# Two layers of window attention on one core: six q, k and v stacks, eight input tiles, one transfer of row maxima per unit, and a new table of slots

## The chip, the cores and the metric

The kernel runs on one NeuronCore of one Trainium2 chip. The metric is the device time of one execution in microseconds, from which the median of several runs is taken. A profiled execution has a time of its own; inside it lies the span, from the first to the last instruction of the core. TensorE has two clock levels, 1.2 and 2.4 GHz; the profile gives the granted one as a share of the upper (0.50 or 1.00, or a mean over a stretch).

## The reference, cut to what matters

There are 64 samples of 14x14 tokens with 192 channels, and two layers of the same kind. Each layer normalises groups of channels, makes q, k and v for 12 heads of 16 channels, adds relative position terms for rows and columns to the scores, takes the softmax over all 196 keys, and projects. The input is added to the result.

```python
qkv = hidden_states.reshape(B, HW, C) @ qkv_w.T + qkv_b
...
attn = jnp.einsum('bqd,bkd->bqk', q * scale, k)
rel_h = jnp.einsum('bhwc,hkc->bhwk', qr, Rh)
rel_w = jnp.einsum('bhwc,wkc->bhwk', qr, Rw)
attn = attn.reshape(B * nh, H, W, H, W) + rel_h[:, :, :, :, None] + rel_w[:, :, :, None, :]
attn = jax.nn.softmax(attn.astype(jnp.float32), axis=-1).astype(q.dtype)
out = jnp.einsum('bqk,bkd->bqd', attn, v)
out = out @ proj_w.T + proj_b
...
x = x + _L0_conv_ref(_gn(x), ...)
x = x + _L1_conv_ref(_gn(x), ...)
```

## The kernel before

**Units, slots, iterations.** One sample in one layer is a unit; there are 128. Every engine walks through the same iterations, and an iteration has 12 slots, one for each head. A step has a number, its place: a step at place 46 of unit n is done in slot 46 mod 12 = 10 of the iteration that lies 46 div 12 = 3 after the one of n. So the steps of some six units stand beside each other in one iteration, and in each iteration each step is done once, for some unit. The order of the instructions of an engine is fixed by the places and, within a slot, by the order in which the code asks for them. What an engine needs from another it waits for on a semaphore; all waits block the engine's own queue.

**The steps of a unit.** SP loads the input into `xa`; TensorE transposes it (`xT`); DVE and POOL make the statistics (`bn`, `mv`, `group`), with one small matmul `g` between them; POOL normalises and splits into two halves of 16 bits (`xn`, `xhi`, `xlo`). TensorE makes q and k (`qk0`, `qk1`) and v (`v`). ACT and DVE split q and k into `qk_hl`; SP writes them to DRAM (`qk_out`) and reads them back in another layout into the stacks `q_st` and `k_st` (`q_in`, `k_in`). The matmuls `rel0`, `rel1`, `rel2` make the position terms from `q_st`; ACT and DVE split them into `rel_hl`, and SP copies that into more rows of `q_st` (`rel`, four transfers).

**The two score passes.** For each head `ps_max` = q times k without the last row is made at MAX_AT + head (L525); DVE reduces it to the row maximum in `mx` (L718). TensorE transposes `mx` (`mT0` for the first six heads, `mT1` for the others, L480), ACT scales it into `mrow`, and SP copies `mrow` into the last row of `q_st` (`m0` and `m1`, L337). Then the same product with the last row, `ps_sc`, at EXP_AT + head (L538), has the maximum subtracted, and ACT takes the exponential into `probs` (L588). The matmul for head 0 waits for `m0` and that for head 6 waits for `m1`.

**The rest.** `ps_o` = v times probs (PV_AT, L557); ACT copies it to `o_sb`; `ot`, `on`, `oT` and `y` divide, transpose and project; POOL adds the input, which SP has loaded a second time into `xd`, and SP writes the result (`out`).

**Banks.** The jobs of TensorE other than L525, L538 and L557 share three PSUM banks. JOBS gives for each its place, name, bank and what tells that its bank has been read. `bank_free` lets a job wait until the job before it in the same bank has been read.

**Buffers.** `q_st`, `k_st` and `v_st` have four buffers each, `xa`, `xd`, `mrow` and most others two. SP's queue goes, in each iteration: `xa` (slot 0), `m0`, `qk_out`, `q_in` (slot 3), `k_in` (4), `xd` (7), `out` (9), `m1`, `rel` (10).

Of the kernel before, what the change touches and what calls it, by code (L numbers as in the profile page):

```python
# [58 lines left out]
UNROLL = 4  # L59

# [11 lines left out]
def attention_kernel(nc, x_in, w_all, b_qk, b_rows, rel, onehot, lo_rows, ident_in, gmat_in, out):  # L72
    with ExitStack() as ctx:
# [37 lines left out]
        q_st = [sb(f"q_st{i}", [128, HEADS, 2, HT], F16) for i in range(4)]  # L111
        k_st = [sb(f"k_st{i}", [128, HEADS, TOK], F16) for i in range(4)]
        v_st = [sb(f"v_st{i}", [HT, 2, HEADS, PW]) for i in range(4)]
# [5 lines left out]
        xa = pair("xa", [HT, 2, C])  # L119
# [18 lines left out]
        mrow = pair("mrow", [HEADS, 2, HT], F16)  # L138
# [6 lines left out]
        xd = pair("xd", [HT, 2, C])  # L145
# [52 lines left out]
        s_m = [sems(f"s_m{h}_") for h in range(2)]  # L198
# [13 lines left out]
        s_xd = sems("s_xd")  # L212
# [39 lines left out]
        JOBS = [(60, "y", 0, (s_yr, 1, 1)),  # L252
                (3, "qk0", 1, (s_qklo, 2, 1)),
                (3, "qk1", 0, (s_qklo, 2, 2)),
                (-9, "xT", 2, (s_xT, 1, 1)),
                (17, "rel0", 0, (s_rlo, 3, 1)),
                (41, "mT1", 2, (s_mrow, 2, 2)),
                (18, "rel1", 1, (s_rlo, 3, 2)),
                (-5, "g", 2, (s_g, 1, 1)),
                (56, "ot", 0, (s_on, 1, 1)),  # L260
                (20, "rel2", 1, (s_rlo, 3, 3)),
                (58, "oT", 2, (s_olo, 1, 1)),
                (10, "v", 0, (s_v, 1, 1)),
                (35, "mT0", 1, (s_mrow, 2, 1))]
# [44 lines left out]
        def _(sp):  # L309
# [36 lines left out]
            def iteration(unit, layer):  # L346
                for s in range(HEADS):
                    for half in range(2):
                        u = due(unit, s, SP_AT[f"m{half}"])
                        if u:  # L350
                            maxima(u, half)
                    u = due(unit, s, SP_AT["rel"])
                    if u:
                        wait(sp, s_rlo, u.n * 3 + 3)
                        for axis in range(2):
                            rows = RW if axis == 0 else 2 * SIDE
                            for half in range(2):
                                p, r0 = 64 * axis + 32 * half, R_REL + RW * axis
                                sp.dma_start(q_st[u.r][r0:r0 + rows, half * HH:half * HH + HH, :, :],
                                             rel_hl[u.r % 2][p:p + rows, :, :]).then_inc(s_rel[u.r], 16)  # L360
# [18 lines left out]
                    u = due(unit, s, SP_AT["xd"])
                    if u:  # L380
                        src, at = (x_in, u.n) if not layer_of(u, layer) else (x1, u.n - SAMPLES)
                        wait(sp, s_y, u.n - 1)
                        sp.dma_start(xd[u.r % 2][:, :, :], tokens(src[bass.ds(at, 1)])).then_inc(s_xd[u.r], 16)  # L383
# [6 lines left out]
                    if u:  # L390
# [3 lines left out]
                        wait(sp, s_xT_ps, u.n - 1)  # L394
                        sp.dma_start(xa[u.r % 2][:, :, :], tokens(src[bass.ds(at, 1)])).then_inc(s_x[u.r], 16)
# [7 lines left out]
        def _(pe):  # L403
# [14 lines left out]
            def job(name, unit, slot, layer):  # L418
# [6 lines left out]
                if name == "xT":  # L425
                    wait_dma(pe, s_x, u)
                    bank_free(pe, unit, name)
                    for c in range(2):
                        for h in range(2):
                            last = nc.tensor.transpose(ps[0:CC, c * TOK + h * HT:c * TOK + h * HT + HT],  # L430
                                                       xa[p2][:, h, c * CC:c * CC + CC], ident[0:HT, 0:HT])
# [20 lines left out]
                elif name.startswith("rel"):  # L452
# [7 lines left out]
                    for i in range(SIDE):  # L460
                        for axis in range(2) if i < rows else (1,):
                            w = 2 * (SIDE - 1 - (i if axis else a0 + i))
                            for half in range(2):
# [3 lines left out]
                                q = q_st[u.r][0:R_REL, half * HH:half * HH + HH, :, :]\  # L467
# [46 lines left out]
            def iteration(unit, layer):  # L514
                for s in range(HEADS):
# [3 lines left out]
                    if u:  # L519
# [394 lines left out]
```

## Time and profile before

| | |
|---|---|
| median of 3 runs | 2550.9 us (2547.81 to 2555.18) |
| the profiled execution | 2526.95 us |
| its span | 2525.2 us |
| TensorE busy in the span | 2178.0 us, 86% |
| VectorE (DVE) | 1434.6 us, 57% |
| ScalarE (ACT) | 1419.7 us, 56% |
| GpSimd (POOL) | 715.6 us, 28% |
| DMA, share of 16 engines | 33.8% |

The busy time of an engine is that of its instructions, whatever the clock, so TensorE's busy time holds matmuls at either level. The idle time in front of a group of instructions is put down to what released it. Names of tiles stand without their buffer number.

### The profile page before, as it was taken

The page shows a single profiled execution, that of the slowest core. Times are in us where ns is not written, and L with a number is a line of the kernel's source. Part 1 is how long each engine was busy: PE and PEld are TensorE (multiplying, and loading weights), DVE is VectorE, ACT ScalarE, POOL GpSimd, SP SyncE. Part 2 cuts the span into 40 slices and gives each one's busy share as a digit, 9 for nine tenths or more (in the row PEclk, how much of TensorE's full clock was granted, in tenths as well). Part 3 has the DMA queues.
Part 4 walks back from the last instruction along what each step waited for, and adds up shares of the span by engine and source line. Part 5 has one row for each costly group of instructions (what it writes and reads, how often), then busy time and mean ns, then how long its engine had stood idle before and what let it go on. Part 6 is the DMA issues. An engine that isn't in the chain of part 4 may idle for free.

```text
span 2525.2 us, 86928 instructions
## 1 busy us (share of the span) xinstructions
PE 2178.0 (86%) x35072; PEld 1815.6 (72%) x35072; DVE 1434.6 (57%) x3540; ACT 1419.7 (56%) x3329; POOL 715.6 (28%) x1796
## 2 busy tenths in 40 slices
PE   2888888888988888988988888988888888898897
PEld 2777777777777777776777777777777777777776
DVE  5655555565555556555555555655555655565554
ACT  1556555555655555655555555555555655565555
POOL 1322322232223223223222322332223222323220
PEclk9989888888888989989888988888888988998888
DMA  2433333333333334333333433333333333333331
GB/s 49 106 85 84 93 85 85 83 98 87 80 85 90 92 81 100 86 85 98 84 80 85 101 81 80 90 92 85 80 90 95 85 87 81 96 90 88 89 78 52
DMA packets 170599, 217.20 MB, mean 86 GB/s; under 512 B 29783, under 2 KB 138072, under 8 KB 170202
## 3 DMA queue, kind: packets, MB, share of 16 engines
q1 hardware_dynamic: 170202, 211.64, 33.8%
q8 instruction: 282, 4.62, 0.8%
q14 instruction: 115, 0.94, 0.1%
HBM read 117.00 MB, written 57.80 MB: 69 GB/s over the span
## 4 chain that ended last, share of the span: by engine, by line
PE 42%; DMA 30%; SPq 16%; DVE 5%; issue 3%; ACT 3%; POOL 1%; POOLq 0%; ACTq 0%
PE ps_m L413 21%; DMA q_st<-mrow 14%; DMA k_dram<-qk_hl 10%; PE ps_sc L538 8%; SPq L376 7%; PE ps_max L525 6%; DMA q_dram<-qk_hl 5%; DVE qk_hl L730 4%; SPq L383 3%; PE ps_m L501 3%; SPq L388 3%; PE ps_o L557 3%; ACT qk_hl L600 2%; SPq L342 2%; SPq L370 1%
## 5 line engine op out<-in xcount | busy, mean ns | idle before, releaser
L718 DVE TENSOR_REDUCE mx<-ps_max 98x2 f32<-98x392 f32 x1536 | 836.8, 562 | 433.1 <-PE ps_max L525 431.4
L588 ACT ACTIVATE probs<-ps_sc 98x392 f32<-98x392 f32 x1536 | 727.7, 495 | 536.6 <-PE ps_sc L538 505.5
L538 PE MATMUL ps_sc<-q_st,k_st 125*98 125x196 f16 x3072 | 568.7, 270 | 286.4 <-DMA q_st<-mrow 286.1
L525 PE MATMUL ps_max<-k_st,q_st 124*98 124x196 f16 x3072 | 580.4, 273 | 0.9 <-DVE mx L718 0.7
L538 PEld LDWEIGHTS ps_sc<-q_st,k_st 125*98 125x98 f16 x3072 | 352.7, 137 | 314.3 <-DMA q_st<-mrow 311.6
L525 PEld LDWEIGHTS ps_max<-k_st,q_st 124*98 124x98 f16 x3072 | 324.5, 135 | 204.7 <-issue 198.3
L802 POOL TENSOR_TENSOR msq<-mv 96x2 f32<-96x2 f32 x128 | 24.6, 192 | 1538.2 <-DVE mv L744 1538.2
L557 PE MATMUL ps_o<-probs,v_st 98*32 98x196 f32 x6144 | 389.0, 340 | 0.5 <-ACT o_sb L578 0.5
L636 ACT ACTIVATE rel_hi<-ps_m,is_lo 128x504 f16<-128x504 f32 (+1 forms) x384 | 225.8, 588 | 149.4 <-PE ps_m L474 137.3
L776 DVE TENSOR_TENSOR oT_lo<-ps_m,oT_hi 96x392 f16<-96x392 f32 x128 | 71.9, 562 | 415.5 <-ACT oT_hi L618 415.5
L474 PE MATMUL ps_m<-q_st,rel_st 64*32 64x36 f16 (+1 forms) x14336 | 238.2, 209 | 1.9 <-DVE rel_hl L769 1.6
L769 DVE TENSOR_TENSOR rel_hl<-ps_m,rel_hi 128x504 f16<-128x504 f32 (+1 forms) x384 | 216.2, 563 | 23.2 <-ACT rel_hi L636 6.5
L474 PEld LDWEIGHTS ps_m<-q_st,rel_st 64*32 64x32 f16 x14336 | 191.5, 101 | 46.1 <-DVE rel_hl L769 2.3
L413 PE MATMUL ps_m<-xn_hi,w_hi 98*128 98x196 f16 (+1 forms) x768 | 193.2, 252 | 10.4 <-POOL xn_lo L844 10.4
L413 PE MATMUL ps_m<-xn_lo,w_hi 96*128 96x196 f16 x768 | 192.2, 250 | 0.0
L730 DVE TENSOR_TENSOR qk_hl<-ps_m,qk_hl 128x392 f16<-128x392 f32 (+1 forms) x256 | 107.2, 460 | 149.5 <-ACT qk_hl L600 149.5
L413 PE MATMUL ps_m<-xn_hi,w_lo 96*128 96x196 f16 x768 | 191.6, 249 | 0.0
L557 PEld LDWEIGHTS ps_o<-probs,v_st 98*32 98x32 f32 x6144 | 134.4, 108 | 73.2 <-issue 1.0
L413 PE MATMUL ps_m<-w_hi,xn_lo 96*98 96x192 f16 x512 | 176.0, 344 | 0.0
L413 PE MATMUL ps_m<-w_lo,xn_hi 96*98 96x192 f16 x512 | 175.8, 343 | 0.0
L413 PE MATMUL ps_m<-w_hi,xn_hi 98*98 98x192 f16 (+1 forms) x512 | 175.6, 343 | 0.0
L413 PE MATMUL ps_m<-w_hi,oT_hi 98*98 98x192 f16 (+1 forms) x512 | 154.0, 301 | 2.7 <-DVE oT_lo L776 2.7
(72 smaller groups left out, 3338.3 us busy)
## 6 DMA issues: line engine op xcount, KB each, us to landing
q_st<-q_dram SPq DMA_DIRECT2D x128, 294.0 KB, 3.9
k_st<-k_dram SPq DMA_DIRECT2D x256, 147.0 KB, 3.9
q_dram<-qk_hl SPq DMA_DIRECT2D x128, 147.0 KB, 2.6
k_dram<-qk_hl SPq DMA_DIRECT2D x128, 147.0 KB, 2.7
q_st<-rel_hl SPq DMA_DIRECT2D x256, 73.5 KB
q_st<-rel_hl SPq DMA_DIRECT2D x256, 64.3 KB
xa<-in_x SPq DMA_DIRECT2D x64, 147.0 KB
xd<-in_x SPq DMA_DIRECT2D x64, 147.0 KB
```

Of the source, the lines that this page charges most:

```text
L376: sp.dma_start(k_st[u.r][2 * HD * part:2 * HD * part + 2 * HD, :, :], k_dram[u.r].rearrange("l d h c t -> d l (h c t)"))\
L383: sp.dma_start(xd[u.r % 2][:, :, :], tokens(src[bass.ds(at, 1)])).then_inc(s_xd[u.r], 16)
L413: last = nc.tensor.matmul(dst, weights(a, c, k), moving(b, c, k), start=n == 0, stop=n == len(terms) - 1)
L474: last = nc.tensor.matmul(to, rel_st[:, lay, axis, w:w + RW], q, start=True, stop=True)
L525: last = nc.tensor.matmul(ps_max[head % 2][0:HT, h * TOK:h * TOK + TOK], q_st[u.r][0:R_MAX, head, h, :], k_st[u.r][0:R_MAX, head, :], star ...
L538: last = nc.tensor.matmul(ps_sc[head % 2][0:HT, kt * TOK:kt * TOK + TOK], k_st[u.r][0:STACK, head, kt * HT:kt * HT + HT], q_st[u.r][0:STAC ...
L557: last = nc.tensor.matmul(ps_o[32 * j:32 * j + 32, 0:TOK], v_st[u.r][:, kt, head_of(head), :], p[:, kt, :], start=kt == 0, stop=kt == 1)
L588: nc.scalar.activation(probs[head][:, :, :], ps_sc[head % 2][0:HT, 0:2 * TOK].rearrange("p (k t) -> p k t", k=2), ACT.Exp, scale=1.0 / (QS ...
L636: nc.scalar.activation(rel_part(rel_hi[u.r % 2], n), rel_bank(n), ACT.Identity, scale=is_lo[:, 0:1]).then_inc(s_rhi, 1)
L718: nc.vector.reduce_max(mx[u.r % 2][:, head, :], ps_max[head % 2][0:HT, 0:2 * TOK].rearrange("p (q k) -> p q k", q=2), axis=AX.X).then_inc( ...
L730: nc.vector.tensor_tensor(qk_hl[u.r % 2][:, 1, at, :], ps_m[BANK[f"qk{j}"]][:, 0:len(tiles) * TOK].rearrange("p (c t) -> p c t", t=TOK), q ...
L769: nc.vector.tensor_tensor(rel_part(rel_hl[u.r % 2], n), rel_bank(n), rel_part(rel_hi[u.r % 2], n), ALU.subtract).then_inc(s_rlo, 1)
```

## The change

- `q_st`, `k_st` and `v_st` get six buffers, used in turn by the unit's number modulo six.
- `xa` gets eight buffers and is kept until POOL has added it to the result; the second load, `xd`, goes. A load of `xa` now waits for POOL's addition for the unit eight before it.
- The maxima of all 12 heads are transposed at once (`mT`, 24 rows in place of 12 twice), scaled by one ACT instruction and copied by one transfer, `m`. The matmul L538 waits for it at head 0 alone.
- All places are new: MAX_AT from 28 to 30, EXP_AT from 40 to 47, the jobs with their banks, the steps of POOL and SP. LEAD goes from 1 to 2, so there is one more iteration.
- At the start DVE fills two more `v_st` and the constant rows of two more `k_st`.

```diff
+VB = 6
+QB = 6
+XB = 8
...
-        LEAD, TAIL = 1, 6
-        MAX_AT, EXP_AT = 28, 40
-
-        PV_AT = {(0, 0): 44, (0, 1): 45, (1, 0): 49, (1, 1): 51, (2, 0): 54, (2, 1): 54}
+        LEAD, TAIL = 2, 6
+        MAX_AT, EXP_AT = 30, 47
+
+        PV_AT = {(0, 0): 52, (0, 1): 52, (1, 0): 55, (1, 1): 56, (2, 0): 59, (2, 1): 61}
...
-        JOBS = [(60, "y", 0, (s_yr, 1, 1)),
-                (3, "qk0", 1, (s_qklo, 2, 1)),
...
-                (41, "mT1", 2, (s_mrow, 2, 2)),
...
-                (35, "mT0", 1, (s_mrow, 2, 1))]
+        JOBS = [(-10, "xT", 1, (s_xT, 1, 1)),
+                (63, "ot", 0, (s_on, 1, 1)),
+                (4, "qk0", 2, (s_qklo, 2, 1)),
+                (5, "qk1", 1, (s_qklo, 2, 2)),
+                (65, "oT", 2, (s_olo, 1, 1)),
+                (18, "rel0", 0, (s_rlo, 3, 1)),
+                (42, "mT", 1, (s_mrow, 1, 1)),
+                (19, "rel1", 2, (s_rlo, 3, 2)),
+                (68, "y", 1, (s_yr, 1, 1)),
+                (-4, "g", 2, (s_g, 1, 1)),
+                (22, "rel2", 2, (s_rlo, 3, 3)),
+                (10, "v", 0, (s_v, 1, 1))]
...
-        POOL_AT = {"mv": -11, "group": -3, "xn": -1, "xhi": 0, "xlo": 0, "y": 63}
+        POOL_AT = {"mv": -8, "group": -5, "xn": -5, "xhi": -1, "xlo": 3, "y": 72}
...
-        SP_AT = {"m0": 39, "m1": 46, "rel": 22, "qk_out": 3, "q_in": 3, "k_in": 4, "xd": 55, "out": 69, "xa": -12}
+        SP_AT = {"m": 44, "rel": 23, "qk_out": 6, "q_in": 9, "k_in": 9, "out": 73, "xa": -22}
...
+                    u = due(unit, s, SP_AT["m"])
+                    if u:
+                        wait(sp, s_mrow, u.n + 1)
+                        sp.dma_start(q_st[u.n % QB][R_MAX:STACK, :, :, :], mrow[u.r % 2][:, :])\
+                          .then_inc(s_m[u.r], 16)
...
-                        wait(sp, s_xT_ps, u.n - 1)
-                        sp.dma_start(xa[u.r % 2][:, :, :], tokens(src[bass.ds(at, 1)])).then_inc(s_x[u.r], 16)
+                        wait(sp, s_y, u.n - XB + 1)
+                        sp.dma_start(xa[u.n % XB][:, :, :], tokens(src[bass.ds(at, 1)])).then_inc(s_x[u.r], 16)
...
-                        if head % HH == 0:
-                            wait_dma(pe, s_m[head // HH], u)
+                        if head == 0:
+                            wait_dma(pe, s_m, u)
...
-                        nc.gpsimd.tensor_tensor(yo[p2][:, :, :], yr[p2][:, :, :], xd[p2][:, :, :], ALU.add)\
+                        nc.gpsimd.tensor_tensor(yo[p2][:, :, :], yr[p2][:, :, :], xa[u.n % XB][:, :, :], ALU.add)\
```

On SP's queue, this is one iteration in the middle of the program before, with what each transfer waits for:

```order
L337 DMA q_st<-mrow 1x12x98 [waits s_mrow]
L342 DMA q_dram<-qk_hl 64x2x588 [waits s_qklo]
L342 DMA k_dram<-qk_hl 64x2x588
L370 DMA q_st<-q_dram 64x1x2352 [waits s_qd0]
L376 DMA k_st<-k_dram 32x1x2352 [waits s_kd0]
L376 DMA k_st<-k_dram 32x1x2352
L383 DMA xd<-in_x 98x2x192 [waits s_y]
L388 DMA x<-yo 98x2x192 [waits s_y]
L337 DMA q_st<-mrow 1x12x98 [waits s_mrow]
L359 DMA q_st<-rel_hl 32x1176 [waits s_rlo]
```

And this is one iteration of the same queue in the changed kernel:

```order
L335 DMA q_dram<-qk_hl 64x2x588 [waits s_qklo]
L335 DMA k_dram<-qk_hl 64x2x588
L344 DMA q_st<-mrow 1x24x98 [waits s_mrow]
L364 DMA q_st<-q_dram 64x1x2352 [waits s_qd0]
L370 DMA k_st<-k_dram 32x1x2352 [waits s_kd0]
L370 DMA k_st<-k_dram 32x1x2352
L353 DMA q_st<-rel_hl 32x1176 [waits s_rlo]
```

The second transfer of maxima stood behind the write of q and k to DRAM, their way back, `xd` and `out`; now the only one stands directly behind the write.

On DVE, before, these are the slots 2 to 6 of an iteration, from the reduction (L718) ahead of the split of q and k (L730) over the statistics (L739 to L744) to the position terms (L769):

```order
L730 TENSOR_TENSOR qk_hl<-ps_m,qk_hl 128x392 [waits s_kd0,s_qd0,s_qkhi]
L730 TENSOR_TENSOR qk_hl<-ps_m,qk_hl 128x196 [waits s_qkhi]
L718 TENSOR_REDUCE mx<-ps_max 98x2 [waits s_mT_ps,s_sm_ps]
L718 TENSOR_REDUCE mx<-ps_max 98x2 [waits s_sm_ps]
L739 BN_STATS bn<-xT 96x6 [waits s_xT]
L739 BN_STATS bn<-xT 96x6
L742 MEMSET anchor 96x1 [waits s_g_ps,s_bn]
L744 BN_AGGR mv<-bn 96x2 x2
L769 TENSOR_TENSOR rel_hl<-ps_m,rel_hi 128x6x84 [waits s_rhi,s_rel3]
```

In the changed kernel these are slots 5 to 8 on DVE (L713 is the split of q and k, L759 that of `oT`, L752 that of the position terms, L767 the copy after `g`):

```order
L701 TENSOR_REDUCE mx<-ps_max 98x2 [waits s_sm_ps]
L713 TENSOR_TENSOR qk_hl<-ps_m,qk_hl 128x196 [waits s_qkhi]
L759 TENSOR_TENSOR oT_lo<-ps_m,oT_hi 96x392 [waits s_y_ps,s_ohi]
L701 TENSOR_REDUCE mx<-ps_max 98x2 [waits s_mT_ps,s_sm_ps]
L752 TENSOR_TENSOR rel_hl<-ps_m,rel_hi 128x6x84 [waits s_rhi,s_rel3]
L701 TENSOR_REDUCE mx<-ps_max 98x2 [waits s_sm_ps]
L752 TENSOR_TENSOR rel_hl<-ps_m,rel_hi 128x6x84 [waits s_rhi]
L701 TENSOR_REDUCE mx<-ps_max 98x2 [waits s_sm_ps]
L767 COPY gsm<-ps_m 96x4 [waits s_gp,s_g_ps]
```

The split of `oT` now stands between that of q and k and those of the position terms, and four of the steps read or free the same bank 2.

## Rows read from the trace of the kernel before

**Rows 1.** The page: the span, its busy times and the clock in 40 slices.

```profile
span 2525.2 us, 86928 instructions
PE 2178.0 (86%) x35072; PEld 1815.6 (72%) x35072; DVE 1434.6 (57%) x3540; ACT 1419.7 (56%) x3329; POOL 715.6 (28%) x1796
PEclk9989888888888989989888988888888988998888
```

**Rows 2.** Who waited for whom: engine, tile, releaser, us, times, longest.

```profile
PE ps_sc L538 <- DMA q_st<-mrow: 286.1, 125, 3.7
```

**Rows 3.** Windows: length, busy time of each engine, granted clock, DMA.

```profile
108.88:125.14 16.26, 14.95 (x275) 12.14 (x275) 10.92 (x27) 10.83 (x26) 5.52 (x15) 1.00 0.40 105
125.14:2508.00 2382.86, 2099.26 (x33910) 1753.21 (x33910) 1362.26 (x3332) 1376.17 (x3231) 680.69 (x1699) 0.87 0.35 87
...
1219.00:1220.00 1.00, 1.00 (x8) 1.00 (x7) 0.47 (x1) 0.48 (x1) 0.00 (x0) 0.50 0.34 82
```

**Rows 4.** TensorE in order of time: start, length, what, [idle before].

```profile
1215.90 0.37 PE L525 MATMUL ps_max<-k_st,q_st 124*98 124x196 f16 x2
1217.77 0.56 PE L538 MATMUL ps_sc<-q_st,k_st 125*98 125x196 f16 x2 [1.50 <-DMA q_st<-mrow]
```

**Rows 5.** SP's queue in order of time, 1209 to 1216 us.

```profile
1209.63 0.64 SPq L342 DMA_DIRECT2D k_dram<-qk_hl  x1
1211.51 0.56 SPq L370 DMA_DIRECT2D q_st<-q_dram  x1
1212.46 1.96 SPq L376 DMA_DIRECT2D k_st<-k_dram  x2
1214.46 0.57 SPq L383 DMA_DIRECT2D xd<-in_x  x1
...
1215.53 0.81 SPq L337 DMA_DIRECT2D q_st<-mrow  x1
```

**Rows 6.** TensorE in order of time, pieces of two stretches at clock 1.00.

```profile
93.89 0.25 PE L413 MATMUL ps_m<-w_hi,xn_hi 98*98 98x192 f16 x1
...
94.89 0.33 PE L525 MATMUL ps_max<-k_st,q_st 124*98 124x196 f16 x2
...
1208.27 0.54 PE L557 MATMUL ps_o<-probs,v_st 98*32 98x196 f32 x8
1208.74 0.37 PE L525 MATMUL ps_max<-k_st,q_st 124*98 124x196 f16 x2
...
1209.56 0.67 PE L474 MATMUL ps_m<-q_st,rel_st 64*32 64x84 f16 x40
1210.15 0.25 PE L480 MATMUL ps_m<-ident,mx 98*12 98x98 f32 x1
```

**Rows 7.** From issue to landing of `k_st`, from the view of line L376.

```profile
DMA to landing us min/median/max: 2.8/3.9/5.0
```

**Rows 8.** Groups by line: busy us, mean ns | idle before, releaser.

```profile
L718 DVE TENSOR_REDUCE mx<-ps_max 98x2 f32<-98x392 f32 x1536 | 836.8, 562 | 433.1 <-PE ps_max L525 431.4
...
L769 DVE TENSOR_TENSOR rel_hl<-ps_m,rel_hi 128x504 f16<-128x504 f32 (+1 forms) x384 | 216.2, 563 | 23.2 <-ACT rel_hi L636 6.5
```

**Rows 9.** POOL in order of time: from the statistics to the split input.

```profile
1231.08 1.01 POOL L855 TENSOR_TENSOR yo<-yr,xd 98x384 f32<-98x384 f32 x1
1233.08 0.19 POOL L812 TENSOR_TENSOR msq<-gsm 96x2 f32<-96x2 f32 x1 [1.00 <-DVE gsm L784]
...
1236.88 0.93 POOL L844 TENSOR_TENSOR xn_lo<-xn,xn_hi 96x392 f16<-96x392 f32 x1
```

**Rows 10.** The start: DVE's fills, TensorE's first step, the first L538.

```profile
3.89 3.12 DVE L668 MEMSET v_st<- 98x768 f32 x4 [0.20 <-issue]
...
7.45 5.99 DVE L675 COPY k_st<-oh_f 61x196 f16<-61x196 f16 x48
...
33.22 0.89 PE L430 MATMUL ps_m<-ident,xa 98*96 98x98 f32 x4 [33.22 <-DVE yo L707]
...
85.49 0.53 PE L538 MATMUL ps_sc<-q_st,k_st 125*98 125x196 f16 x2
```

More of the change, by code:

```diff
@@ L108, in attention_kernel @@
         anchor = sb("anchor", [CC, 3])
-        q_st = [sb(f"q_st{i}", [128, HEADS, 2, HT], F16) for i in range(4)]
-        k_st = [sb(f"k_st{i}", [128, HEADS, TOK], F16) for i in range(4)]
-        v_st = [sb(f"v_st{i}", [HT, 2, HEADS, PW]) for i in range(4)]
+        q_st = [sb(f"q_st{i}", [128, HEADS, 2, HT], F16) for i in range(QB)]
+        k_st = [sb(f"k_st{i}", [128, HEADS, TOK], F16) for i in range(QB)]
+        v_st = [sb(f"v_st{i}", [HT, 2, HEADS, PW]) for i in range(VB)]
         def pair(name, shape, dt=F32):
             return [sb(f"{name}{i}", shape, dt) for i in range(2)]
-        xa = pair("xa", [HT, 2, C])
+        xa = [sb(f"xa{i}", [HT, 2, C]) for i in range(XB)]
         xT = pair("xT", [CC, 2, TOK])
@@ L137, in attention_kernel @@
         mx = pair("mx", [HT, HEADS, 2])
-        mrow = pair("mrow", [HEADS, 2, HT], F16)
+        mrow = pair("mrow", [2 * HEADS, HT], F16)
         probs = [sb(f"probs{i}", [HT, 2, TOK]) for i in range(HEADS)]
@@ L197, in attention_kernel @@
         s_mrow = sem("s_mrow")
-        s_m = [sems(f"s_m{h}_") for h in range(2)]
+        s_m = sems("s_m")
         s_sc_ps = sem("s_sc_ps")
@@ L347, in iteration @@
                 for s in range(HEADS):
[L348 to L351, printed above, removed]
+                    u = due(unit, s, SP_AT["m"])
[3 more added lines that the diff above has]
+                          .then_inc(s_m[u.r], 16)
                     u = due(unit, s, SP_AT["rel"])
@@ L375, in iteration @@
                         for part in range(2):
-                            sp.dma_start(k_st[u.r][2 * HD * part:2 * HD * part + 2 * HD, :, :],
+                            sp.dma_start(k_st[u.n % QB][2 * HD * part:2 * HD * part + 2 * HD, :, :],
                                          k_dram[u.r].rearrange("l d h c t -> d l (h c t)"))\
                               .then_inc(s_kst[u.r], 16)
[L379 to L383, printed above, removed]
                     u = due(unit, s, SP_AT["out"])
@@ L602, in iteration @@
                                            .rearrange("p (c t) -> p c t", t=TOK)).then_inc(s_qkhi, 1)
-                    for half in range(2):
-                        name = f"mT{half}"
-                        u = due(unit, s, AT[name] + ACT_LATER["mT"])
-                        if u:
-                            act.wait_ge(s_mT_ps, u.n * 2 + half + 1)
-                            before = unit((AT[name] + ACT_LATER["mT"]) // HEADS + 2)
-                            if active(before):
-                                wait_dma(act, s_m[half], before)
-                            nc.scalar.activation(mrow[u.r % 2][:, half, :], ps_m[BANK[name]][0:HEADS, 0:HT],
-                                                 ACT.Copy, scale=-1.0 / KS).then_inc(s_mrow, 1)
+                    u = due(unit, s, AT["mT"] + ACT_LATER["mT"])
+                    if u:
+                        act.wait_ge(s_mT_ps, u.n + 1)
+                        before = unit((AT["mT"] + ACT_LATER["mT"]) // HEADS + 2)
+                        if active(before):
+                            wait_dma(act, s_m, before)
+                        nc.scalar.activation(mrow[u.r % 2][:, :], ps_m[BANK["mT"]][0:2 * HEADS, 0:HT],
+                                             ACT.Copy, scale=-1.0 / KS).then_inc(s_mrow, 1)
                     u = due(unit, s, AT["oT"] + ACT_LATER["oT"])
@@ L640, in iteration @@
                         act.wait_ge(s_v_ps, u.n + 1)
-                        wait(act, s_o_ps, (u.n - 3) * GROUPS)
-                        nc.scalar.copy(v_st[u.r][:, :, :, 0:HD],
+                        wait(act, s_o_ps, (u.n - VB + 1) * GROUPS)
+                        nc.scalar.copy(v_st[u.n % VB][:, :, :, 0:HD],
                                        ps_m[BANK["v"]][0:HT, 0:2 * C]
@@ L666, in _ @@
                 nc.vector.memset(oT_hi[i][CC:CB, :, :], 1.0)
-            for i in range(UNROLL):
+            for i in range(VB):
                 nc.vector.memset(v_st[i][:, :, :, :], VS)
@@ L672, in _ @@
             dve.wait_ge(s_oh, 1)
-            for i in range(UNROLL):
+            for i in range(QB):
                 for head in range(HEADS):
```

48 lines of the change are left out of this document (14 added, 34 removed).

## The prediction, made before the changed kernel had run

> **What bounds the kernel now.** I read four views, in this order. The page first: TensorE is busy 86% of the span, DVE and ACT 57% and 56%, so none is full on average [rows 1]. Then the waits: on TensorE one line stands for nearly all idle time, L538 waiting for the transfer of the maxima, 286.1 us in 125 waits, 2.29 us each, one per unit [rows 2]. Then the windows. Between 108.88 and 125.14 us lies one full period, from the sixth-head wait of one unit to that of the next: 16.26 us, 14.95 of them busy, at clock 1.00. From 125.14 to 2508 us lie the 125 periods to unit 127's wait: 2382.86 / 125 = 19.06 us each, 2099.26 / 125 = 16.79 busy, 2.27 idle, at clock 0.87 [rows 3]. The same instructions take 1.84 us more of busy time, because for a part of every period TensorE runs at the lower level, 1.2 GHz [rows 3]: the wait that ends at 1217.77 is followed by a window at 0.50, with 8 matmuls in a microsecond [rows 3, 4]. So a period is 14.95 of work at 2.4 GHz, 2.27 of wait and 1.84 of what the wait leaves behind. The clock stays up with 1.31 us idle in the period (16.26 less 14.95) and falls in the period with 1.50 of wait [rows 3, 4].
>
> Last SP's queue, for why the maxima come late. `m1` is issued at 1215.53, and L538 goes on at 1217.77, 2.24 us later [rows 4, 5]. The transpose of an `mT` had begun at 1210.15 [rows 6]; from there the maxima lie ready, but SP is in the middle of the way of q and k over DRAM: the write at 1209.63, `q_in` at 1211.51 when the write has landed, `k_in` at 1212.46 for 1.96 us, `xd` at 1214.46, then `out`, then `m1` [rows 5]. The limit is a round trip through one in-order queue; no wait in the views is for a free stack.
>
> **The change part by part.**
>
> *The place of the maxima.* In the new table SP has only `qk_out` ahead of `m` in the half period that matters. I lay the period out from the start of slot 6 at clock 1.00, with pieces from rows: a group of PV 0.47 (1208.27 to 1208.74), a pair L525 and L538 0.41 with the changes of type (1208.74 to 1209.56 holds two), a `rel0` or `rel1` 0.59, a job of 12 split matmuls 1.0 (93.89 to 94.89) [rows 6]. `mT` begins after one pair and `rel0`, at 1.0. To the L538 of head 0 in slot 11 TensorE has: `rel1` 0.6, PV 0.5, `y` 1.0, `g` 0.1, PV 0.5, `rel2` 0.5, `v` 1.0, and four pairs and a half, 1.8. Sum 6.0, so head 0 is due at 7.0. ACT is at `mrow` at about 2.5 (it has the exponential of slot 6, the copy of `rel0` and the exponential of slot 7 ahead of it), SP issues at 2.6. With 2.24 from issue to use [rows 4, 5] the maxima are there at 4.8; with the longest landing of a far larger transfer, 5.0 [rows 7], at 7.6. I take the first, since it is this transfer, with 24 rows in place of 12. The stall of 2.27 goes whole; what is late next is nothing by 2.2 us. At the other bound 0.6 us of it stays.
>
> The Trainium skill (DMA: Bandwidth & Descriptors, section "Why a DMA increments its semaphore by 16 and not by 1") says that the first dimension of both sides sets over how many engines a transfer is split, the largest number up to 16 that divides both: by that 6 before (12 rows, 6 heads) and 12 now (24 rows, 12 heads), so landing would not be later and the sum stays. No row shows a transfer of 24.
>
> *The clock.* With no wait over 1.31 us left, the level stays up as in the stretch of 16.26 us, and the 1.84 goes too [rows 3]. Bounds: 1.84 back, or nothing back.
>
> *Work on TensorE.* One transpose less of 0.1 us; all else is the same. Period: 14.95 less 0.09 = 14.86.
>
> *Small new waits.* DVE has 10.92 us of work in a period, ACT 10.83 [rows 3], against 14.86, so neither is a bound on average; but slots 4 to 8 hold most of DVE's. I walk DVE through them with 0.56 for a reduction and about 0.63 for a long split of `rel` [rows 8]. It finishes the split of `qk1` at 0.8, where `mT` (same bank 1) wants to begin at 1.0; that of `oT` at 1.35, where `rel1` (same bank 2) wants 1.5; that of `rel1` at 3.9, where `g` (bank 2) wants 4.0. Three near ties, each with 0.1 to 0.2 us in hand. `g` also holds up the second half of PV behind it, and any such loss is a loss of the period. From below: 0. From above: each tie lost by one reduction that comes first, 0.56 us, some 1.1 for two of them. I take 0.1 us a period, since every tie falls on the good side.
>
> *POOL.* From `group` to `xlo` it takes 4.7 us (1233.08 to 1237.81), and the addition 1.0 [rows 9] now stands between `xhi` and `xlo`. Group starts at about 4.6, so `xlo` is done at 10.4 and `qk0` is due in slot 4, at 11.7: covered, 1.3 us in hand. If that cover went, `qk0` would wait, with everything behind it.
>
> *SP.* `xd` (0.57) and one of the two `m` (0.8) go [rows 5]. What moves: `q_in` and `k_in` to slot 9, nine slots ahead of `rel0`; `rel` to slot 11, four issues of about 0.7 each from 6.9 to 9.8, needed by L525 of head 0 at 14.86 + 0. With 3.9 to land 13.7, with 5.0 14.8 [rows 7]: just covered at both. `out` and `xa` now wait for POOL's addition, done at 9.4, and behind them in the queue is `qk_out`, due at 15.7: covered by 6 us. Six and eight buffers cost no time in the loop: they let a stack live from place 9 to 58, over four periods, which four buffers would not.
>
> *Start and end.* Two more `v_st` at 0.78 each and 24 more copies at 0.125 are 4.6 us ahead of TensorE's first step [rows 10]. From there to the first L538 it took 52.3 us for 49 places [rows 10]; now it is 57 places. At the same rate 8.5 us more; but the loop of the fill is freer (the transpose of the next unit no longer stands behind `qk0`), so between 0 and 8.5. I take 5. The end is of the same length.
>
> **Sum**, against the profiled execution: 125 x (19.06 - 14.86) = 525, and 3 for the two first periods (two waits of 1.3): 2525.2 - 528 = 1997. Plus 4.6, plus 5, plus 125 x 0.1 = 13: span 2020. The execution lies 1.75 above its span: 2022. The median before is 24 us above its profiled execution, which I put down mostly to the wait and the clock, which vary from period to period; 3 us of that stay: **2025 us**, 21% faster.
>
> **The rivals.**
>
> *Ties lost.* One or two of the bank waits on DVE bind in every period, for 0.2 to 1.1 us: 2050 to 2150 us. For it: DVE in slots 4 to 8 has next to no gap, and the walk sets no latency aside for semaphores. Against it: DVE's dense part now ran next to TensorE without waits of TensorE that the views would show but one.
>
> *The maxima come late in part.* Landing at 5 us: 0.6 us a period, 2100 us with the clock up. For it: one transfer now serves head 0 as well, so every head depends on it, and it shares the engines with the write of k. Against it: 2.24 us measured among heavier traffic [rows 4, 5].
>
> *The clock does not stay up.* Tiny waits, one at each near tie, would hold TensorE at the lower level for as long as now: 1.84 x 125 = 230, so 2255 us. Against it: the stretch with 1.31 us idle stayed at 1.00 [rows 3]. The Trainium skill (TensorE: Matmul & The Clock Gate, section "A second HAM failure mode: psum-queue depth-cycling") describes short idles between groups of matmuls as banks are cycled, which make the clock swing although no wait is long. By that rule this rival comes true; the trace so far speaks for the other.
>
> *Slower.* A single transfer of 24 rows into one partition that takes much longer to land. It is issued at 2.6 and due at 7.0, so anything over 4.4 us is a wait, and a wait over about 1.5 brings the lower clock with 1.84 back. The gain is gone when the wait reaches 4.2 - 0.2 - 1.84 = 2.2 us, at a landing of 6.6 us; at 8 us the time is 2025 + 125 x (3.6 + 1.84) = 2705 us. Nothing in the trace lands so late.
>
> *It does not do what it says.* If the first six heads' maxima, which now wait for the last six, were the late ones, the old wait would only have moved from head 6 to head 0. The layout above gives them 4.4 us; it is the same case as the one of late maxima.
>
> **How the numbers follow.** Forecast (2000 to 2050) 0.66; ties lost 0.18; maxima late in part 0.06; clock not up 0.07; slower 0.03. The range reaches down to the case without small waits and with a free start (2022 - 13 - 5, less some 15 for a shorter period) and up over the ties lost: 1988 to 2155 us, which leaves out about 0.15. A difference under 0.3% can't be told from none. Faster 0.96, same 0.01, slower 0.03.
>
> **What would show it.** In the new trace L538 should have no wait for the maxima, or under 20 us in all; the granted clock should be 1.00 in windows of the middle; a period should be 14.9 to 15.0; `m` should be issued directly behind the write of k. Small waits of TensorE for DVE at `mT`, `rel1` or `g` would show the ties lost. A clock near 0.9 without waits over a microsecond would show the third rival. I would be wrong if one engine's queue that I laid out by hand carried a wait that I took as covered: POOL's 1.3 us and the landing of `rel` are the thinnest.

## The result, and the profile after

The changed kernel takes 1973.1 us (median of 4 runs, 1971.98 to 1974.22) against 2553.0 before (four runs; the table ahead of the prediction has three of them): a ratio of 0.773, interval 0.771 to 0.775. I had forecast 2025 us, range 1988 to 2155. The direction and the mechanism held, but the time lies 52 us under the forecast and 15 under the range.

The page of the changed kernel, its busy times, the clock, the chain that ended last:

```profile
span 1971.3 us, 85928 instructions
PE 1904.9 (97%) x34944; PEld 1558.5 (79%) x34944; DVE 1436.1 (73%) x3566; ACT 1364.7 (69%) x3201; POOL 713.3 (36%) x1796
PEclk9999999999999999999999999999999999999999
PE 93%; issue 3%; DVE 2%; POOL 1%; ACT 0%; DMA 0%; POOLq 0%; SPq 0%; DVEq 0%; ACTq 0%
```

Beside [rows 1]: TensorE went from 86 to 97% of the span and its busy time fell by 273 us (2178.0 to 1904.9), for the same work less 128 transposes. Most of that is the half speed which went, 1.84 us in each of 125 periods or 230 us; the rest is the transposes and the tails of matmuls in front of waits (see the period of 14.86 below). In the chain, 30% was DMA and 16% SP's queue before, and now both are at 0%. The chain before was:

```profile
PE 42%; DMA 30%; SPq 16%; DVE 5%; issue 3%; ACT 3%; POOL 1%; POOLq 0%; ACTq 0%
```

The line of [rows 2] is not there any more: no L524 waits for the maxima, in any of 128 units.

Windows of the middle, columns as in [rows 3]:

```profile
800.00:1200.00 400.00, 400.00 (x7414) 327.78 (x7412) 298.61 (x733) 290.01 (x682) 153.38 (x384) 1.00 0.42 104
1205.51:1220.19 14.68, 14.68 (x280) 12.04 (x273) 10.97 (x28) 10.63 (x26) 5.57 (x14) 1.00 0.42 105
```

400 us with 400 us busy, at clock 1.00; the second line is one period, from `mT` to `mT`: 14.68 us. SP's queue in that period:

```profile
1205.20 0.67 SPq L335 DMA_DIRECT2D q_dram<-qk_hl  x1
1205.91 0.63 SPq L335 DMA_DIRECT2D k_dram<-qk_hl  x1
1206.93 0.80 SPq L344 DMA_DIRECT2D q_st<-mrow  x1
1207.95 0.59 SPq L364 DMA_DIRECT2D q_st<-q_dram  x1
1208.68 1.66 SPq L370 DMA_DIRECT2D k_st<-k_dram  x2
1211.32 2.88 SPq L353 DMA_DIRECT2D q_st<-rel_hl  x4
```

The maxima are issued at 1206.93, between the write of q and k and their way back; before, `m1` came after all of it [rows 5]. TensorE and POOL at the places that the prediction walked through (start, length, what):

```profile
1204.92 0.66 PE L463 MATMUL ps_m<-q_st,rel_st 64*32 64x84 f16 x40
1205.51 0.26 PE L468 MATMUL ps_m<-ident,mx 98*24 98x98 f32 x1
...
1208.48 0.26 PE L425 MATMUL ps_m<-mv,gmat 96*96 96x4 f32 x2
...
1211.60 0.33 PE L524 MATMUL ps_sc<-q_st,k_st 125*98 125x196 f16 x2
```

```profile
1209.01 0.19 POOL L795 TENSOR_TENSOR msq<-gsm 96x2 f32<-96x2 f32 x1 [4.02 <-DVE gsm L767]
...
1213.67 0.93 POOL L827 TENSOR_TENSOR xn_lo<-xn,xn_hi 96x392 f16<-96x392 f32 x1
```

The slot began at 1204.48, so `mT` is at 1.0, the issue of the maxima at 2.45 and head 0 at 7.1 (laid out by hand: 1.0, 2.6, 7.0).

### The profile page after: what moved, and what is told of

It reads as the page before. It is cut to its first block, busy times and chain, and to the rows that moved or that the text cites. A ratio compares the mean times of both kernels' runs of the same rounds, so it can differ in the third digit from the quotient of the medians.

```text
span 1971.3 us, 85928 instructions
## 1 busy us (share of the span) xinstructions
PE 1904.9 (97%) x34944; PEld 1558.5 (79%) x34944; DVE 1436.1 (73%) x3566; ACT 1364.7 (69%) x3201; POOL 713.3 (36%) x1796
## 4 chain that ended last, share of the span: by engine, by line
PE 93%; issue 3%; DVE 2%; POOL 1%; ACT 0%; DMA 0%; POOLq 0%; SPq 0%; DVEq 0%; ACTq 0%
PE ps_m L402 24%; PE ps_max L511 17%; PE ps_o L543 17%; PE ps_sc L524 13%; PE ps_m L463 10%; PE ps_m L477 6%; PE ps_m L419 2%; PE ps_m L487 2%; PE ps_m L468 1%; PE ps_m L425 1%; DVE k_st L658 0%; POOL yo L837 0%; DVE v_st L651 0%; POOL xn L814 0%; POOL xn_lo L827 0%
## 5 line engine op out<-in xcount | busy, mean ns | idle before, releaser
L511 PE MATMUL ps_max<-k_st,q_st 124*98 124x196 f16 x3072 | 538.1, 257 | 0.6 <-DVE mx L701 0.3
L524 PE MATMUL ps_sc<-q_st,k_st 125*98 125x196 f16 x3072 | 511.7, 247 | 0.6 <-ACT probs L574 0.5
L511 PEld LDWEIGHTS ps_max<-k_st,q_st 124*98 124x98 f16 x3072 | 293.8, 125 | 200.1 <-issue 157.6
L524 PEld LDWEIGHTS ps_sc<-q_st,k_st 125*98 125x98 f16 x3072 | 320.9, 124 | 3.4 <-ACT probs L574 1.8
L752 DVE TENSOR_TENSOR rel_hl<-ps_m,rel_hi 128x504 f16<-128x504 f32 (+1 forms) x384 | 216.2, 563 | 85.5 <-ACT rel_hi L619 85.5
L795 POOL TENSOR_TENSOR msq<-gsm 96x2 f32<-96x2 f32 x128 | 24.6, 192 | 505.4 <-DVE gsm L767 505.4
L713 DVE TENSOR_TENSOR qk_hl<-ps_m,qk_hl 128x392 f16<-128x392 f32 (+1 forms) x256 | 117.1, 457 | 78.9 <-ACT qk_hl L586 78.9
L564 ACT COPY o_sb<-ps_o 128x196 f32<-128x196 f32 x384 | 123.9, 323 | 59.5 <-PE ps_o L543 47.2
L586 ACT CAST qk_hl<-ps_m 128x392 f16<-128x392 f32 (+1 forms) x256 | 103.5, 404 | 84.5 <-PE ps_m L402 82.8
L477 PE MATMUL ps_m<-ident,o_sb 128*98 128x68 f32 x1536 | 150.7, 246 | 0.4 <-ACT o_sb L564 0.4
L837 POOL TENSOR_TENSOR yo<-yr,xa 98x384 f32<-98x384 f32 x128 | 128.6, 1005 | 57.5 <-ACT yr L633 57.5
```

What stands on the lines that cost most here:

```text
L477: last = nc.tensor.matmul(ps[0:HT, at:at + HG * (HD + 1)], o_sb[p2][:, g, h * HT:h * HT + HT], ident[:, :].rearrange("p (j x) -> p j x", x ...
L524: last = nc.tensor.matmul(ps_sc[head % 2][0:HT, kt * TOK:kt * TOK + TOK], k_st[u.n % QB][0:STACK, head, kt * HT:kt * HT + HT], q_st[u.n % ...
L564: nc.scalar.copy(o_sb[u.r % 2][:, g, :].rearrange("p (k r b) -> p k r b", r=2, b=SIDE), ps_o[:, 0:TOK].rearrange("p (k b r) -> p k r b", r ...
L752: nc.vector.tensor_tensor(rel_part(rel_hl[u.r % 2], n), rel_bank(n), rel_part(rel_hi[u.r % 2], n), ALU.subtract).then_inc(s_rlo, 1)
L837: nc.gpsimd.tensor_tensor(yo[p2][:, :, :], yr[p2][:, :, :], xa[u.n % XB][:, :, :], ALU.add)\
```

## The experiments

**1. The kernel before, with the way back of q and k behind the second transfer of maxima.**

```diff
-        SP_AT = {"m0": 39, "m1": 46, "rel": 22, "qk_out": 3, "q_in": 3, "k_in": 4, ...
+        SP_AT = {"m0": 39, "m1": 43, "rel": 22, "qk_out": 3, "q_in": 8, "k_in": 8, ...
```

> The kernel before, with nothing changed but three numbers of SP's table: m1 from place 46 to 43 (slot 7), q_in from 3 to 8 and k_in from 4 to 8 (slot 8). The way back of q and k from DRAM then stands behind the second transfer of maxima; four buffers, xd, two transposes and all other places stay. Theory (the place in SP's queue is the cause of the wait, and the wait of the low clock): no wait for the maxima, clock 1.00, a period of 14.8 us, about 1975 us. Rival (it needs the buffers, the kept input or the new table of slots): the wait only goes over to another step, 2300 to 2550 us.

Measured: 1975.5 us, ratio 0.775 (0.772 to 0.778), 2 us from the changed kernel. The page and SP's queue:

```profile
PE 1910.9 (97%) x35072; PEld 1567.9 (79%) x35072; DVE 1424.7 (72%) x3540; ACT 1387.2 (70%) x3329; POOL 715.1 (36%) x1796
```

```profile
1206.92 0.65 SPq L342 DMA_DIRECT2D k_dram<-qk_hl  x1
1208.87 0.78 SPq L337 DMA_DIRECT2D q_st<-mrow  x1
1209.70 0.53 SPq L383 DMA_DIRECT2D xd<-x  x1
1210.28 0.57 SPq L370 DMA_DIRECT2D q_st<-q_dram  x1
```

`m1` now stands directly behind the write of k. No L538 waits for the maxima any more, and the clock is 1.00 in every window between 400 and 1900 us. Three numbers in one table give the whole gain; none of it needs six buffers, the kept input, the single row or the other slots. The rival is out. The changed kernel has a period that is 0.07 us shorter (14.70 on average against 14.76, `mT` to `mT` in the two traces), but its first matmul with the maximum comes some 10 us later (95.4 against 85.7 us), and the two about cancel.

**2. The same kernel, with `m1` alone moved** (46 to 43; `q_in` and `k_in` stay at 3 and 4).

> The kernel before, with m1 alone moved, from place 46 to 43: it then stands ahead of xd and out, but still behind q_in and k_in. Both theories expect the wait to shorten by the issues of xd and out, 1.07 us a period. If the clock depends on the length of the wait (it held with 1.31 us idle in a period), it comes back in most periods: 2525 - 134 - 230 = 2160 us. If any wait of about a microsecond keeps it low: 2390 us.

Measured: 2246.9 us, 0.881 (0.875 to 0.886), between the two expectations. The waits for the maxima are 165.7 us in 126 (from 286.1), so 0.97 us less each. That is worth some 120 us; the time fell by 305. The rest is the clock, which came back in a part of the periods. Two windows, each from the end of one wait to the end of the next:

```profile
1226.73:1244.99 18.26, 17.85 (x274) 15.08 (x274) 10.79 (x27) 11.15 (x26) 4.10 (x12) 0.83 0.39 105
...
1261.17:1276.82 15.65, 14.95 (x274) 12.13 (x274) 10.93 (x27) 10.83 (x26) 5.13 (x14) 1.00 0.40 101
```

The waits that opened them, in TensorE's order of time:

```profile
1226.73 0.56 PE L538 MATMUL ps_sc<-q_st,k_st 125*98 125x196 f16 x2 [2.08 <-DMA q_st<-mrow]
...
1261.17 0.37 PE L538 MATMUL ps_sc<-q_st,k_st 125*98 125x196 f16 x2 [1.24 <-DMA q_st<-mrow]
```

274 matmuls in both; 17.85 us busy after a wait of 2.08, and 14.95 after one of 1.24.

**3. The changed kernel, with its maxima behind `q_in` and `k_in`** (`"m": 44` to `46`).

> The changed kernel, with its one transfer of maxima at place 46 in place of 44, so behind q_in and k_in on SP's queue. It is issued some 3.5 us later, lands at about 1212.6 by the clock of the changed kernel's trace, and L524 of head 0 is due at 1211.6: a wait of 1.0 us a period. Theory (queue place sets the wait, clock holds at waits of a microsecond): 1973 + 127 = 2100 us, clock over 0.97. If six buffers or the new slots absorb it: 1975 us. If the clock falls at a microsecond: 2330 us.

Measured: 2432.8 us, 0.953 (0.948 to 0.958). So six buffers and new slots hide nothing of it: the same place in the queue brings most of the old time back. But I had expected 2100. The waits are 242.8 us in 125, 1.94 each and not 1.0, and the clock is 0.90. The miss is the time from issue to use. In one period:

```profile
1217.72 1.23 SPq L370 DMA_DIRECT2D k_st<-k_dram  x2
1218.99 0.83 SPq L344 DMA_DIRECT2D q_st<-mrow  x1
1220.54 3.30 SPq L353 DMA_DIRECT2D q_st<-rel_hl  x4
```

```profile
1223.07 0.56 PE L524 MATMUL ps_sc<-q_st,k_st 125*98 125x196 f16 x2 [2.09 <-DMA q_st<-mrow]
...
1300.55 0.37 PE L524 MATMUL ps_sc<-q_st,k_st 125*98 125x196 f16 x2 [1.23 <-DMA q_st<-mrow]
```

Here it is 4.08 us from issue to use (1218.99 to 1223.07), with 588 KB of q and k issued directly ahead of it. But one case says little, for this time varies widely. From the starts of all issues and of the matmuls that waited for them, in the traces:

| kernel | issued directly ahead | issue to use, us: lowest, median, highest | cases |
|---|---|---|---|
| before | `xd` and `out`, 147 KB each | 1.94, 2.89, 4.38 | 125 |
| experiment 3 | `q_in` and `k_in`, 588 KB | 2.26, 3.30, 5.02 | 125 |
| experiment 4 | four `rel`, 64 to 74 KB each | 1.95, 1.97, 2.12 | 126 |

So the 2.24 of [rows 4, 5], on which my 1.0 us of wait rested, was a low case of its own kernel. With the median of 3.30 in its place the wait comes to 2.1 us, near the 1.94 measured. And again the level goes with the wait: the first window below follows a wait of 2.25, the second the one of 1.23.

```profile
1281.81:1300.55 18.74, 17.50 (x274) 13.83 (x274) 11.06 (x27) 11.11 (x25) 4.52 (x14) 0.84 0.31 77
1300.55:1316.77 16.22, 14.90 (x274) 12.05 (x274) 10.97 (x27) 10.74 (x25) 5.64 (x15) 1.00 0.37 95
```

For all periods between 400 and 1400 us that lie between two such waits, this is the mean clock, by the wait that opened the period:

| kernel | after waits up to 1.4 us | after longer ones |
|---|---|---|
| experiment 2 | 36 periods, clock 0.99 | 22 periods, 0.88 |
| experiment 3 | 16 periods, 0.98 | 37 periods, 0.88 |
| before | 2 periods, 0.91 | 49 periods, 0.87 |

There is no sharp border. The trace of before has a wait of 1.28, ended at 1029.63, with a period at 0.91 behind it, and then one of 2.40, ended at 1048.54, with a period at 1.00. Seven of the 108 periods behind a wait over 1.4 us had the full level.

**4. The changed kernel, with its maxima behind `rel` as well** (`"m": 48`; one run).

> The changed kernel, with the transfer of maxima at place 48, behind q_in, k_in and the four transfers of rel. Theory: issued at about 1214.2 in the period of the trace, landing at 1216.5, where 1211.6 is due: a wait of 4.9 us a period, and the low level after it as in the kernel before. 1973 + 622 + 234 = 2830 us, clock about 0.85. If the low clock comes from something else than waits, about 2600 us with clock 1.00.

Measured: 2889.8 us, span 2888.0, clock 0.829, waits 581.4 us in 126, 4.6 each. This is the slower rival made real. By its price for a wait of 4.6 us (2025 + 125 x (4.6 + 1.84)) it would be 2830 us; the 60 us more mean that the lower clock costs more than 1.84 behind such waits. From issue to use it is 1.96 us here, behind the four `rel` transfers (issued 1214.57, used 1216.53):

```profile
1214.57 0.74 SPq L344 DMA_DIRECT2D q_st<-mrow  x1
...
1216.53 0.57 PE L524 MATMUL ps_sc<-q_st,k_st 125*98 125x196 f16 x2 [4.44 <-DMA q_st<-mrow]
```

**5. The changed kernel with two transposes and two transfers of maxima.**

```diff
+                    for half in range(2):
+                        last = nc.tensor.transpose(ps[0:HEADS, half * HT:half * HT + HT],
+                                                   mx[p2][:, HH * half:HH * half + HH, :]...
...
+                        for half in range(2):
+                            sp.dma_start(q_st[u.n % QB][R_MAX:STACK, half * HH:half * HH + HH, :, :],
+                                         mrow[u.r % 2][:, half, :]).then_inc(s_m[u.r], 16)
```

> The changed kernel with its maxima in two halves again, at the same place: two transposes of 12 rows into one bank, one ACT instruction, two transfers behind each other. TensorE gets one matmul of 0.09 us more in a period. If TensorE is full in every period (theory): +0.09 x 127 = 11 us, 1984 us. If there is slack: 1973 us. If the second transfer comes too late: over 2000 us.

Measured: 1983.6 us (1982.6 to 1984.9), 10.5 more than the changed kernel. The period went from 14.70 to 14.78 us on average, so one matmul of 0.09 us in a period shows nearly in full: TensorE is the bound, and the single row is worth 10 us.

**6. Five stacks in place of six** (`VB = 5`, `QB = 5`).

> The changed kernel with five q, k and v stacks in place of six. A stack lives from place 9 to 58, 49 places or 4.1 periods, so five are enough. Theory: the loop is as fast, the start is shorter by 12 copies of 0.125 us and one fill of 0.78: 1971 us. If the sixth keeps a wait away: 1990 us or more.

Measured: 1971.0 us (1970.6 to 1972.0), 2 less, which is 0.1% and no gain to count on. The sixth stack keeps no wait away; it costs its filling at the start (the first L524 comes at 92.6 us in place of 95.4).

**7. The second load back.**

```diff
+        SP_AT = {"m": 44, ..., "xd": 64, "out": 73, "xa": -22}
...
-  nc.gpsimd.tensor_tensor(yo[p2][:, :, :], yr[p2][:, :, :], xa[u.n % XB][:, :, :], ALU.add)\
+  nc.gpsimd.tensor_tensor(yo[p2][:, :, :], yr[p2][:, :, :], xd[p2][:, :, :], ALU.add)\
```

> The changed kernel with the second load of the input, xd, back (place 64, slot 4), and used for the sum in place of the kept tile. One more transfer of 147 KB and one more issue of 0.57 us on SP in every period. Theory (neither SP nor the DMA engines are near the path): 1973 us, within 4. Rival (the second load was a part of what delayed the kernel): over 1985 us.

Measured: 1973.6 us (1973.3 to 1974.2), no change. Keeping the input for the sum is worth nothing here.

**8. The halves of PV together.**

```diff
-        PV_AT = {(0, 0): 52, (0, 1): 52, (1, 0): 55, (1, 1): 56, (2, 0): 59, (2, 1): 61}
+        PV_AT = {(0, 0): 52, (0, 1): 52, (1, 0): 55, (1, 1): 55, (2, 0): 60, (2, 1): 60}
```

> The changed kernel with the two halves of each group of PV in one slot: places 55, 55 and 60, 60 in place of 55, 56 and 59, 61. In the trace a group of 16 matmuls takes 0.81 us, two of 8 take 0.47 each with 0.13 around each for the change of the tile's shape. If TensorE is full and these changes cost what the rows show: 0.49 us less in a period, 1973 - 62 = 1911 us. If DVE or ACT, with 10.97 and 10.63 us in a period, bind where slots get short: 1930 to 1970 us.

Measured: 1912.9 us (1911.7 to 1913.8), ratio 0.749 (0.745 to 0.753). A period is 14.20 us by its trace, from `mT` to `mT`:

```profile
1211.97 0.26 PE L468 MATMUL ps_m<-ident,mx 98*24 98x98 f32 x1
...
1213.08 0.87 PE L543 MATMUL ps_o<-probs,v_st 98*32 98x196 f32 x16
...
1226.17 0.26 PE L468 MATMUL ps_m<-ident,mx 98*24 98x98 f32 x1
```

**9. That, with five stacks and `rel2` beside PV** (`rel2` at place 24, its transfers at 25).

> The changed kernel with five stacks, the halves of PV together (55, 55 and 60, 60), and rel2 at place 24 in place of 22 (slot 0, directly ahead of the PV of that slot; its transfers at 25): the rows of PV and of rel use the same shape of tile, so one more change into and out of it, 0.13 us, goes. If TensorE stays full: 1911 (1973 less 62 and 2) less 0.13 x 127 = 17: 1895 us. If DVE or ACT now bind in the short slots 11, 1 and 2: 1905 to 1930 us.

Measured: 1897.4 us (1896.4 to 1899.7), 0.746 (0.743 to 0.749): faster than both kernels, and 76 us under the changed one. The 0.13 us of a change of shape is there, at 0.11 (a period of 14.09, 1214.34 to 1228.43 by its trace).

**10. The kernel before with experiment 1's numbers and its halves of PV together** (45, 45 and 51, 51).

> The kernel before with the three numbers of SP's table (m1 43, q_in 8, k_in 8) and the halves of PV together (45, 45 and 51, 51 in place of 44, 45 and 49, 51): four buffers, xd, two transfers of maxima, the old table for all else. 1975.5 less two changes of shape of some 0.26 us each in 127 periods, 66: 1910 us, within 10, if TensorE is full there as well. If the four buffers or the old slots have less in hand than the new ones: over 1930 us.

Measured: 1976.1 us (1970.2 to 1977.2), 0.776 (0.773 to 0.780): nothing gained, 66 us off. Its period is 14.79 us on average between 400 and 1800 us, against 14.76 in experiment 1. Three things ate the gain. The group moved from 44 to 45 had stood directly behind `rel2`, with no change of shape ahead of it, so 0.13 was never there. In some periods the transposes of the input now wait for its load `xa`, which kept TensorE idle for 3.6 us between 400 and 1800 us; 23 of 95 periods are over 14.8 us, most of them for it. And slots 1, 2 and 3 are now bare in front of their jobs. TensorE and DVE there:

```profile
1203.34 0.33 PE L525 MATMUL ps_max<-k_st,q_st 124*98 124x196 f16 x2
1203.51 0.33 PE L538 MATMUL ps_sc<-q_st,k_st 125*98 125x196 f16 x2
1203.68 0.33 PE L525 MATMUL ps_max<-k_st,q_st 124*98 124x196 f16 x2
1203.85 0.33 PE L538 MATMUL ps_sc<-q_st,k_st 125*98 125x196 f16 x2
1204.33 0.37 PE L525 MATMUL ps_max<-k_st,q_st 124*98 124x196 f16 x2
```

```profile
1203.71 1.60 DVE L718 TENSOR_REDUCE mx<-ps_max 98x2 f32<-98x392 f32 x3 [0.79 <-PE ps_max L525]
```

A bare slot takes TensorE 0.34 us and DVE's reduction over 0.5; with two banks, the third L525 in a row comes 0.48 us after the L538 ahead of it (1203.85 to 1204.33) where 0.17 is its pace. The list of waits leaves that out, since the last matmul's tail covers half of it, but the windows show that TensorE idles. This one has 5.74 of its 400 us idle, at clock 1.00:

```profile
400.00:800.00 400.00, 394.26 (x7395) 333.07 (x7395) 292.31 (x729) 291.64 (x701) 149.76 (x378) 1.00 0.45 114
```

In the changed kernel every L511 that directly follows an L524 starts 0.17 us behind it, so no wait of this kind is hidden there.

**11 and 12. One layer alone**, for the changed kernel and for that before: 64 units, the second layer left out, the first writing the output.

```diff
-UNITS = LAYERS * SAMPLES
+UNITS = SAMPLES
...
-  dst, at = (x1, u.n) if not layer_of(u, layer) else (out, u.n - SAMPLES)
+  dst, at = out, u.n
```

> The changed kernel with 64 units in place of 128: the second layer is left out and the first writes the output. It parts the time into periods and a fixed piece. If a middle period is 14.68 us, as one in the trace is (1205.51 to 1220.19): 1973.1 less 64 x 14.68 = 1033.6 us, fixed piece 94 us. If the period is the 14.96 of the prediction, and start and end were what was overrated: 1015.6 us.

> The kernel before with 64 units in place of 128, the second layer left out and the first writing the output. If a middle period is 19.06 us, the average that the prediction used: 2553 less 1220 = 1333 us. If middle periods are longer, about 19.2, and the last few shorter: 1324 us. The difference tells how much of the average came from the short periods at the end.

Measured: 1034.0 us (1032.5 to 1034.3) and 1308.2 us (1288.9 to 1320.2). The first hits: (1973.1 - 1034.0) / 64 = 14.67 us a period and a fixed piece of 95. The second hits neither figure; by it a period of the second half would be 19.45 us, while the trace of before has 19.19 (51 periods, 416.18 to 1394.93). The two layers do not cost the same there, or the wait drifts; runs of one kernel lie 31 us apart, so this one settles nothing.

## Why the prediction was right in its mechanism and missed its range

**What bounds the kernel before:** right. Experiment 1 takes away nothing but the place in SP's queue and gets 1975.5. Experiments 3 and 4 put it back into the changed kernel and get the wait back, longer the later it stands.

**The wait is gone whole, nothing is late next:** right, with no wait for the maxima left. The 2.24 us from issue to use was one low case out of 125 with a median of 2.89 and a highest of 4.38 (the table in experiment 3). It did no harm, because the layout left 4.4 us: in the new trace the issue is at 1206.93 and head 0 at 1211.60, 4.67 us apart, and no unit waited. My bound of 5.0 us covered the spread; the price in the expectation of experiment 3 did not. And the copy of 24 rows is not slow by itself: in experiment 4 it took 1.95 to 2.12 us, where the lowest of the 12 rows before is 1.94.

**The clock comes back:** right, 1.00 through the middle, and the rival in which small waits hold it down is out. That rival had the rule of the Trainium skill on queue cycling (TensorE: Matmul & The Clock Gate, "A second HAM failure mode: psum-queue depth-cycling") behind it. The changed kernel does not test that rule, since its tight bank waits left TensorE no idle time. Experiment 10 does, and does not agree: TensorE idled there for a moment in every period, 5.74 of 400 us, and the clock was 1.00.

**Small new waits, 0.1 us a period:** wrong, there are none. DVE in the dense slots:

```profile
1204.82 0.35 DVE L713 TENSOR_TENSOR qk_hl<-ps_m,qk_hl 128x196 f16<-128x196 f32 x1
1205.19 0.56 DVE L759 TENSOR_TENSOR oT_lo<-ps_m,oT_hi 96x392 f16<-96x392 f32 x1
...
1207.57 0.67 DVE L752 TENSOR_TENSOR rel_hl<-ps_m,rel_hi 128x504 f16<-128x504 f32 x1
```

From the slot's start at 1204.48 they end at 0.7, 1.3 and 3.8, where I had 0.8, 1.35 and 3.9: all three ties keep 0.2 to 0.3 us. The allowance was 13 us, and nothing called for it (0.1 us in each of 125 periods).

**The period, 14.86:** this is the step that failed, mis-sized by 0.18. I took the 14.95 us busy of one full period as its work [rows 3]. But a matmul is counted busy to its end, and the next one in a stream starts before that. In front of a wait this tail stands in the open: the L525 of 1215.90 is busy for 0.37 us [rows 4], but where nothing waits the next matmul starts 0.20 us after such an L525, in the same trace:

```profile
1212.08 0.37 PE L525 MATMUL ps_max<-k_st,q_st 124*98 124x196 f16 x2
1212.28 0.34 PE L538 MATMUL ps_sc<-q_st,k_st 125*98 125x196 f16 x2
```

So the wait was 0.17 longer than its row said and the work 0.17 shorter: 14.78, less 0.09 for the transpose, 14.69. Measured: 14.68 in the period shown, 14.70 on average over 94 periods (411.82 to 1793.33 us), 14.67 by experiment 11. Experiment 1 bears the reading out, with the same matmuls in the same places and no wait: 14.76 on average where the row said 14.95 busy. Over 125 periods this is 20 to 22 us. I read "busy" as "needed".

**125 equal periods:** mis-sized as well. The last units have no q, k, v and position terms of later ones beside them. `mT` of the last four units:

```profile
1910.58 0.26 PE L468 MATMUL ps_m<-ident,mx 98*24 98x98 f32 x1
...
1923.30 0.26 PE L468 MATMUL ps_m<-ident,mx 98*24 98x98 f32 x1
...
1934.48 0.25 PE L468 MATMUL ps_m<-ident,mx 98*24 98x98 f32 x1
...
1945.25 0.26 PE L468 MATMUL ps_m<-ident,mx 98*24 98x98 f32 x1
```

12.7, 11.2 and 10.8 us, together 9.4 less than three periods. I averaged such short periods into the 19.06 of before and then gave all 125 the full new work; 9 us.

**Start and end:** right. The first L524 starts at 95.4 us (forecast 95.1, with 4.15 us of filling for my 4.6), and from the last to the end of the span it is 13.0 (before 12.9).

**The 3 us between profile and median:** not there. The changed kernel's median is its profiled execution (1973.08 and 1973.15), and its runs lie 2 us apart where those before lay 11 apart. What varied was the wait.

The sum of the miss: 13 + 22 + 9 + 3 = 47 of 52; 5 us I can't assign to a row. (One of them is rounding: the terms of the forecast add to a span of 2019.3, which I wrote as 2020.) All four errors lean the same way, and the low end of the range, which had no term for a period shorter than the busy time, was too near.

**The rest of the change:** the parts that I costed at nothing cost nothing or a little, and bring as little: the buffers (experiment 6), the kept input (7), the single row 10 us (5). POOL had 1.4 us in hand (`xlo` ends at 1214.60, `qk0` starts at 1216.03) for my 1.3, and the `rel` transfers were issued at 6.8 to 9.7 for my 6.9 to 9.8.

## What to carry to other kernels

When every period waits for one small transfer, ask first what stands ahead of it in its in-order queue: an issue that itself waits (here the way back from DRAM) holds up everything behind it, and moving it by a few places was worth the whole gain here, where the extra buffers were worth nothing. Take the time to landing from all cases in the trace and not from one. Count a wait that lets TensorE's clock fall twice, once for itself and once for the stretch at half speed that follows. And when taking work from a busy time, take it from starts to starts in a full stream; busy time in front of a wait holds the tail of the last matmul.

## What the runs showed of the hardware

- The lower clock goes with the length of the wait. After waits up to 1.4 us the mean clock was 0.99 and 0.98 in 52 periods of experiments 2 and 3, and after longer ones 0.87 to 0.88 in 108 periods of these and the kernel before. It is a tendency and no border: periods at 1.00 follow waits of up to 2.40 us, and one at 0.91 follows a wait of 1.28. The Trainium skill (TensorE: Matmul & The Clock Gate, "HAM oscillation — how this bites in real kernels") puts the gap to avoid well above that; the measured waits, mostly of 1.5 to 2.5 us, decide.
- From the issue of a copy of 2 to 5 KB to its use took 1.95 to 2.12 us behind four copies within SBUF of 64 to 74 KB each, but 1.94 to 4.38 (median 2.89) behind `xd` and `out` of 147 KB each, and 2.26 to 5.02 (median 3.30) behind 588 KB read from DRAM, always on the same queue. Which of size, kind and time of issue makes the difference was not tested. I had expected a figure that belongs to the transfer.
- Going from full-width matmuls to those of 32 columns and back costs TensorE 0.13 us (0.26 and 0.21 us instead of 0.17 between the starts of neighbours in the changed kernel's trace). Bringing `rel2` beside PV took one such change out and gave 0.11 us of a period (experiment 9). Joining two halves of PV gave 0.24 each time (0.48 for two, experiment 8), since 16 matmuls in one piece also take 0.81 us where two pieces of 8 take 0.47 each.
